# Graph attention with a memory layer on one core: edge ranks and places formed one projection earlier, and the first four permutation groups in a PSUM bank of their own

## The reference

```python
def gnn(n_f, ...):                       # n_f: layer-normed x, 256 x 1024, 8192 edges src, dst
    feat = concatenate([n_f[edge_src], n_f[edge_dst]], axis=1)
    e_hh = relu(feat[:128] @ W_hh + b_hh)
    e_oo = relu(feat[128:768] @ W_oo + b_oo)
    e_ho = relu(feat[768:] @ W_ho + b_ho)          # 7424 edges
    logit = (concatenate([e_hh, e_oo, e_ho]) @ W_a + b_a)[:, 0]
    m = segment_max(logit, edge_dst, 256)
    ex = exp(logit - m[edge_dst])
    alpha = ex / segment_sum(ex, edge_dst, 256)[edge_dst]
    z_f = segment_sum(alpha[:, None] * n_f[edge_src], edge_dst, 256)
    nf2 = concatenate([n_f, z_f], axis=1)
    return concatenate([relu(nf2[:64] @ W_hn + b_hn), relu(nf2[64:] @ W_on + b_on)])

x = x + gnn(layernorm(x), ...)
x = x + ffn(layernorm(x), ...)   # hash, top 4 of 256 memories, 1024 -> 32 -> 1024 each
```

## Time and profile before

| | before |
|---|---|
| median of 3 runs | 803.29 us (800.48 to 803.84) |
| the profiled execution's own time | 800.23 us |
| its span, first to last instruction | 798.5 us |
| outside the span | 1.7 us |
| granted TensorE clock, mean | 0.971 |
| PE busy | 741.0 us (93%) |
| DVE busy | 520.5 us (65%) |
| ACT busy | 347.9 us (44%) |
| POOL busy | 197.1 us (25%) |
| `lo` half, DVE L713 | x104, mean 2291 ns |
| `hi` half, ACT L538 | x104, mean 1910 ns |
| edge tile's dot, DVE L898 | x80, mean 1221 ns |

### The profile page before, as it was taken

How to read it: one execution, slowest core, us unless ns; L and a number is a source line. 1 busy time by engine, 2 the same in 40 slices (tenths; PEclk the granted TensorE clock), 3 DMA queues, 4 the chain that set the end, 5 groups by cost and what they waited for, 6 DMA issues and landing times.

```text
span 798.5 us, 9678 instructions
## 1 busy us (share of the span) xinstructions
PE 741.0 (93%) x3305; PEld 573.3 (72%) x3305; DVE 520.5 (65%) x832; ACT 347.9 (44%) x376; POOL 197.1 (25%) x345
## 2 busy tenths in 40 slices
PE   3999978797979998779999999999999999999998
PEld 3777756585555567548877787888888788888786
DVE  6884986596999999936488645445554544554543
ACT  3735576945634432113453443433443432444330
POOL 8200189998898804000000000000000000000000
PEclk9999999998999999868999999999999999999999
DMA  8783322241020013203823654566444466545411
GB/s 317 291 316 118 134 105 106 106 147 65 1 106 2 2 47 122 106 1 136 284 108 105 214 182 143 197 210 210 142 173 154 161 210 210 184 137 191 149 75 53
DMA packets 50060, 114.22 MB, mean 143 GB/s; under 512 B 2246, under 2 KB 35398, under 8 KB 44907
## 3 DMA queue, kind: packets, MB, share of 16 engines
q1 hardware_dynamic: 49418, 112.95, 39.5%
q0 software_dynamic: 160, 0.66, 0.2%
q10 hardware_dynamic: 448, 0.20, 0.1%
HBM read 112.74 MB, written 1.05 MB: 143 GB/s over the span
## 4 chain that ended last, share of the span: by engine, by line
PE 60%; POOL 20%; DVE 11%; issue 6%; ACT 2%; DVEq 0%; POOLq 0%; ACTq 0%
PE ps L1161 17%; PE ps L1163 17%; PE ps L1162 17%; POOL peak L494 5%; POOL chunk_col L487 5%; POOL oh_src L496 4%; POOL pen L499 4%; DVE wlo L713 3%; PE ps L1131 2%; DVE oh_dst L990 1%; PE ps L1431 1%; PE ps L1464 1%; ACT whi L538 1%; PE ps L1152 1%; PE ps L1197 1%
## 5 line engine op out<-in xcount | busy, mean ns | idle before, releaser
L713 DVE TENSOR_TENSOR wlo<-raw,whi 128x2048 fp32r<-128x2048 f32 x104 | 235.5, 2291 | 86.1 <-ACT whi L538 85.3
L538 ACT ACTIVATE whi<-raw 128x2048 fp32r<-128x2048 f32 x104 | 195.9, 1910 | 105.8 <-PE ps L1163 101.3
L1161 PE MATMUL ps<-whi,nT_hi 128*128 128x512 f32 x424 | 172.5, 407 | 3.6 <-DVE wlo L713 2.4
L1163 PE MATMUL ps<-wlo,nT_hi 128*128 128x512 f32 x424 | 169.3, 399 | 0.0
L1162 PE MATMUL ps<-whi,nT_lo 128*128 128x512 f32 x424 | 168.8, 398 | 0.0
L898 DVE SCALAR_TENSOR_TENSOR ps<-ps,xt 128x1024 f32<-128x1024 f32 x80 | 97.7, 1221 | 11.4 <-PE ps L1197 6.6
L1161 PEld LDWEIGHTS ps<-whi,nT_hi 128*128 128x128 f32 x424 | 80.5, 190 | 24.7 <-DVE wlo L713 3.3
L1161 PE MATMUL ps<-whi,gT_hi 128*128 128x512 f32 x240 | 95.3, 397 | 0.0
L1163 PE MATMUL ps<-wlo,gT_hi 128*128 128x512 f32 x240 | 95.2, 397 | 0.0
L1162 PE MATMUL ps<-whi,gT_lo 128*128 128x512 f32 x240 | 95.1, 396 | 0.0
L1095 DVE TENSOR_TENSOR gw<-act_g,route 128x512 f32<-128x512 f32 x32 | 20.7, 689 | 114.0 <-ACT act_g L676 113.9
(11 more groups left out here) (234 smaller groups left out, 902.0 us busy)
## 6 DMA issues: line engine op xcount, KB each, us to landing
raw<-n_L_ffn_values_down_dram SPq DMA_DIRECT2D x16, 2048.0 KB, 8.2
raw<-in_L_ffn_values_up_dram SPq DMA_DIRECT2D x16, 2048.0 KB, 7.4
raw<-in_L_gnn_W_hh_dram SPq DMA_DIRECT2D x8, 1024.0 KB, 8.8
raw<-in_L_gnn_W_oo_dram SPq DMA_DIRECT2D x8, 1024.0 KB, 5.1
raw<-in_L_gnn_W_ho_dram SPq DMA_DIRECT2D x8, 1024.0 KB, 5.1
raw<-in_L_gnn_W_hn_dram SPq DMA_DIRECT2D x8, 1024.0 KB, 4.9
raw<-in_L_gnn_W_on_dram SPq DMA_DIRECT2D x8, 1024.0 KB, 4.9
xt<-in_x_dram SPq DMA_DIRECT2D x4, 512.0 KB, 5.0
```

Source lines behind the costliest of these rows:

```text
L538: nc.scalar.activation(half(whi, s, j, down), half(raw, s, j, down), ACT.Copy)\
L713: nc.vector.tensor_tensor(half(wlo, s, j, down), half(raw, s, j, down), half(whi, s, j, down).bitcast(F32), ALU.subtract)\
L1161: nc.tensor.matmul(o, a_hi, b_hi, start=start, stop=False)
L1163: return nc.tensor.matmul(o, a_hi, b_lo, start=False, stop=stop)
```

## The change

`rank_edges` and `count_buckets` move up in `project(1, 0)`, after steps 3 and 1; `rank_rows` and `places` move up on their engines, between the halves of `hi(0, 3)` and `lo(0, 3)`. Groups 0 to 3 of the permutation run in `project(1, 1)`, into bank 3, after a wait that its four tables have been read. A new instruction on VectorE, `decode_early`, copies them to the new SBUF tile `part_idx`, and TensorE's second head tile, which overwrites bank 3, waits for that (`part_out`). Head tile i is followed by group i + 3 instead of i - 1; `project(2, 0)` has groups 9 to 14 after its steps 0 to 5. `decode` adds `part_idx` in place of copying. GpSimd makes the head destinations of tiles 3 to 5 behind its groups 5 to 7 instead of ahead of groups 1 to 3. `table_lo(1, 1)` is cut in two with a group's rows between, and the halves of `hi` and `lo` of (0, 4) and (0, 5) are interleaved with groups.

```diff
@@ gpsimd
             for n in range(CHUNKS):
                 if n >= 2:
                     pool.wait_ge(permuted, n - 1)
-                if 1 <= n <= HEAD - 3:
-                    head_destinations(n + 2)
...
                 last.then_inc(srccol_ready, 1)
+                if EARLY + 1 <= n < EARLY + HEAD - 2:
+                    head_destinations(n - 2)
@@ scalar
             hi(1, 2)
+            hi(0, 3, parts=(0,))
             rank_rows()
-            hi(0, 3)
+            hi(0, 3, parts=(1,))
+            destination_columns(0)
+            destination_columns(1)
             table_hi(1, 0)
             hi(1, 3)
-            hi(0, 4)
+            hi(0, 4, parts=(0,))
+            destination_columns(2)
+            hi(0, 4, parts=(1,))
+            destination_columns(3)
             table_hi(1, 1)
-            for n in range(HEAD + 1):
+            destination_columns(4)
+            destination_columns(5)
+            hi(1, 4)
+            for n in range(6, 13):
                 destination_columns(n)
-                if n == 1:
-                    hi(1, 4)
-            for n in range(HEAD + 1, HEAD + 5):
-                destination_columns(n)
-            hi(0, 5)
-            for n in range(HEAD + 5, CHUNKS):
-                destination_columns(n)
+            hi(0, 5, parts=(0,))
+            destination_columns(13)
+            hi(0, 5, parts=(1,))
+            destination_columns(14)
             table_hi(2, 0)
@@ vector
-                nc.vector.tensor_copy(slot_idx16[:], values)
-                nc.vector.tensor_copy(slot_idx[:], values).then_inc(decoded, 1)
+                nc.vector.tensor_tensor(slot_idx16[:], values, part_idx[:], ALU.add)
+                nc.vector.tensor_tensor(slot_idx[:], values, part_idx[:], ALU.add).then_inc(decoded, 1)
+
+            def decode_early():
+
+                dve.wait_ge(permuted, EARLY)
+                nc.vector.tensor_copy(part_idx[:].rearrange("p a w -> p (a w)"), bank(3)[:, 0:2 * WN]).then_inc(part_out, 1)
...
             bucket_counts()
-            lo(0, 3)
+            lo(0, 3, parts=(0,))
+            places()
+            lo(0, 3, parts=(1,))
+            chunk_rows(0)
+            chunk_rows(1)
             table_lo(1, 0)
             lo(1, 3)
-            places()
             head_onehot(1)
             head_onehot(2)
-            chunk_rows(0)
-            chunk_rows(1)
-            table_lo(1, 1)
+            chunk_rows(2)
+            chunk_rows(3)
+            table_lo(1, 1, (0, 1))
+            chunk_rows(4)
+            table_lo(1, 1, (2, 3))
+            decode_early()
             lo(0, 4)
             for i in range(1, HEAD):
                 edge_tile(i, pair_of(i))
                 if i + 2 < HEAD:
                     head_onehot(i + 2)
-                chunk_rows(i + 1)
+                chunk_rows(i + 4)
             lo(1, 4)
-            for n in range(HEAD + 1, HEAD + 5):
+            for n in range(10, 13):
                 chunk_rows(n)
-            lo(0, 5)
-            for n in range(HEAD + 5, CHUNKS):
-                chunk_rows(n)
+            lo(0, 5, parts=(0,))
+            chunk_rows(13)
+            lo(0, 5, parts=(1,))
+            chunk_rows(14)
             decode()
@@ tensor
-                    last = nc.tensor.matmul(bank(6)[:, 0:2 * WN], chunk_row[:, n % 2, j % CHUNK, :],
-                                            chunk_col[:, n % 2, j % CHUNK, :], start=j == 0, stop=j == JT - 1)
+                    last = nc.tensor.matmul(bank(3 if n < EARLY else 6)[:, 0:2 * WN], chunk_row[:, n % 2, j % CHUNK, :],
+                                            chunk_col[:, n % 2, j % CHUNK, :], start=j in (0, EARLY * CHUNK),
+                                            stop=j in (EARLY * CHUNK - 1, JT - 1))
...
+                if k == 1 and h == 0 and c == 1:
+                    count_buckets()
                 if k == 1 and h == 0 and c == 3:
-                    count_buckets()
-                if k == 1 and h == 0 and c == 6:
                     rank_edges()
-                if k == 2 and h == 0:
-                    permute(HEAD - 1 + c)
+                if k == 1 and h == 1 and c == 1:
+                    pe.wait_ge(tablo_ready, 4)
+                    permute(0)
+                if k == 1 and h == 1 and c == 3:
+                    permute(1)
+                if k == 2 and h == 0 and EARLY + HEAD - 1 + c < CHUNKS:
+                    permute(EARLY + HEAD - 1 + c)
...
+                        if k == 1 and (t, c) == (0, C - 1):
+                            permute(2)
+                        if k == 1 and (t, c) == (1, C - 3):
+                            permute(3)
...
                 pe.wait_ge(headdst_pool, i)
+                if i == 2:
+                    pe.wait_ge(part_out, 1)
...
                 gather_head(i)
-                permute(i - 1)
+                permute(EARLY - 1 + i)
             pe.wait_ge(dot_done, HEAD - 1)
             project(2, 0)
-            for n in range(HEAD - 1 + C, CHUNKS):
-                permute(n)
```

More of the change, by code:

```diff
@@ L58 @@
 REGS = 8
+EARLY = 4
 ROW = 80
@@ L173, in gnn_ffn @@
             chunk_gap = sb("chunk_gap", [P, CHUNK, WN], F16, edge)
+            part_idx = sb("part_idx", [P, 2, WN], F16, edge)
         pen_head = segall
@@ L272, in gnn_ffn @@
         permuted = sem("permuted")
+        part_out = sem("part_out")
         decoded = sem("decoded")
@@ L557, in _, with table_hi @@
             hi(0, 2)
-            def table_hi(k, h):
-                for t in range(NT):
+            def table_hi(k, h, tiles=range(NT)):
+                for t in tiles:
                     if t == 0:
@@ L886, in _, with table_lo @@
             lo(0, 2)
-            def table_lo(k, h):
+            def table_lo(k, h, quarters=range(4)):
                 tab = (tab_src, tab_dst)[h]
-                for q in range(4):
+                for q in quarters:
                     at, b = STACK_HI[q], STACK_BLOCK[q]
```

## The result

The changed kernel takes 795.31 us (794.19 to 795.58, four runs) against 803.13 (800.48 to 803.84) for the kernel before: a ratio of 0.9906, interval 0.9882 to 0.993. Run again for the experiments (`e1_after`), it was 794.32 against 804.69, ratio 0.9878, interval 0.9858 to 0.9897. Forecast: 794, range 788 to 800, faster.

What follows compares the result with a forecast made beforehand. The prediction took project(2, 1), not decoded, to move the end. Terms: -1.1 + 3.5 + 5.1 = 7.5, + 1.7 clock = 9.2 us; 791.0 against the profiled run, 794.1 against the median, so 794, range 788 to 800.

Steps and rivals of the forecast that it cites:

- What bounded: Whole kernel: GpSimd writing chunk_col from 119.5 to 153.6 us; the end moves with project(2, 1), not with decoded.
- Sorting: First projection: ranks and places move up, so edges are sorted at 69.2 us instead of 93.4.
- Second projection: From 72.2 us: four early groups added, first head starts at 97.7, 1.1 us later than before.
- Heads: Head tiles with their groups: 26.2 us instead of 29.7, 3.5 gained, a stall of 3.4 and a half clock staying.
- Third projection: project(2, 0) with groups 9 to 14: 25.8 us instead of 30.9, 5.1 gained, the new 2.0 inside.
- Clock: Start of project(2, 1): half clock at 158.9 to 162.3 goes with the idle time, 1.7 us gained.
- idle terms: Second projection, heads and third projection together: -1.1 + 3.5 + 5.1 = 7.5 us gained.
- the new 2.0: Third projection, near 130 us: TensorE waits 2.0 us for chunk_rows(10), which stands behind lo(1, 4) on VectorE.
- Rival 1: Clock falls again in the third projection, at project(2, 1)'s start or elsewhere: 7.5 us gained, 795.8; chance 0.15.
- rival 2: After head 2: 3.4 us stall brings no half clock at 111 (1.7), later stages lose one: 790 to 792; chance 0.15.
- Rivals 3 to 5: VectorE bounding the tables, 797 to 801, 0.12; late sorting, 804 and more, 0.04; edges not ready earlier, inside that 0.04.
- rival 3: Third projection: VectorE's queue makes group 13 or 14 slip 2 to 3 us each; gain 2 to 6; chance 0.12.

Runs made afterwards that it cites:

- e3_bias_spread: Changed kernel with the eight bias matmuls of project(1, 1) spread over steps 4 to 7 of project(1, 0); 794.09 us, ratio 0.9872.
- e6_after_pool: Changed kernel with one more GpSimd instruction per group, writing a tile nobody reads; 799.57 us, ratio 0.9943.
- e4_sorted_early: Kernel before with only ranks and places formed early, no group permuted early; 803.80 us, ratio 1.0004.
- e2_lo_early: Changed kernel with lo(0, 4) moved ahead of table_lo(1, 1) on VectorE; 789.39 us, ratio 0.9814.
- e7_decode_late: Changed kernel with three extra VectorE reductions between the last group and the decoding; 792.43 us, ratio 0.9853.
- e9_both_lo_early: Changed kernel with lo(0, 4) early and first halves of hi(1, 4) and lo(1, 4) between the destination tables' halves; 787.75 us, ratio 0.9801.
- e10_dest_first: Changed kernel with GpSimd's head destinations of tiles 3 to 5 ahead of its columns 5 to 7; 797.98 us, ratio 0.9927.
- e11_two_early: Changed kernel with two groups instead of four in project(1, 1), groups 7 to 14 in project(2, 0); 793.29 us, ratio 0.9886.
- e5_before_pool: Kernel before with one more GpSimd instruction per group, writing a tile nobody reads; 811.12 us, ratio 1.0092.

## Why the prediction was right

**What bounded.** Right. `chunk_col` on GpSimd left the chain, one instruction a group more cost the kernel before 6.6 us, and the end moved with `project(2, 1)` and not with `decoded`: `decoded` came 10 us sooner, the first dot 7.1. That is a tenth more than the 7 below which the prediction was to count as wrong, and 2 us short of the 9.2 forecast.

**Sorting.** The edges were sorted at 69.7, for 69.2 forecast.

**Second projection**, -1.1. It was -2.9: first head at 99.46 for 97.7, the term that was sized worst. 0.5 of the miss is the wait for `tablo_ready`, taken as 0.2, which is 0.72 where the clock holds (`e1_after`); sorting ended 0.5 late, and the columns stand in front of the tables. 0.7 is the half clock in 74.6 to 78.0, which no step had. The other 0.6 is in small pieces; 0.2 of it lie ahead of the projection (bias matmuls at 72.49, before at 72.26).

**Heads**, +3.5. Right to a tenth, 26.2, with the wait of 3.4 (it was 3.23) ended by `chunk_row`, the half clock behind it, and 0.53 at 104.50 for the 0.5. Both mechanisms are shown by undoing them: `lo(0, 4)` moved takes away wait and half clock, destinations moved back bring the old waits back.

**Third projection**, +5.1. 25.9 for 25.8; the new 2.0 is 1.83, the decoding at 146.7 five us before it is asked for. The prediction had GpSimd lose only group 11 to the `lo` pair. It lost the last column of group 10 as well, done at 133.15, and the wait fits because VectorE's rows, at 133.48, came a little later still.

**Clock**, +1.7. The half clock at 158.9 is gone, `project(2, 1)` takes 24.7 for 24.5. But the one at 74.6 came, 0.7 net, so in the profiled pair the term is 0.8, and the dot moved by 7.1, not 9.2. Over many runs the term is larger than I gave it. Runs of the kernel before on the chips of the experiments stand mostly at a mean clock of 0.963 to 0.967 and 803 to 806 us; those few at 0.971 took 800.6 to 800.9. The new kernel is mostly at 0.969 to 0.974, and its two runs at 0.971 took 793.5 and 794.2. At the same clock the change is worth some 6.4 to 7.4 us (the idle terms were 7.5), and the other 3 to 4 of the 10.4 in `e1_after` go with a higher mean clock; no trace of before at 0.963 to 0.967 was kept, so where its clock fell is not shown. The profiled execution of before had a high clock for that kernel. That I set the sum against it, and then moved the result up to the median, made 794 come out close. That closeness is in part luck: the idle terms were 1.2 too large in the profiled pair, the clock term about 2 too small over the runs beside `e1_after`, and the gain by medians was 7.8 us in the first runs and 10.4 in the second, for 9.2 forecast.

**Rivals.** Rival 1 is what the profiled execution shows, by its words "or once more elsewhere": its 7.5 us and 795.8 stand beside 7.1 and 795.31, though the half clock fell where it had not looked. Its other place, behind the new wait of 2.0, shows in `e3_bias_spread` (the fall at 133 behind 1.95). Half of rival 2's condition, the wait of 3 us without a half clock at 111, was met in two variants (3.08 in `e3_bias_spread`, 3.10 in `e6_after_pool`), and the clock fell elsewhere in both, so no time was gained by it. Rivals 3 to 5 did not occur; `e4_sorted_early` shows what is near to 5: sorted early, no early groups, no gain.

**What was argued wrongly though the number held.** "Only GpSimd pays, and early, where its groups have 5 us of slack", and the 3 us of slack a group in rival 3. The first half is right: the changed trace's `lo` pair beside GpSimd takes 4.49, and GpSimd's four destinations 6.42 under it for 2.47 without it. (By the Trainium skill, "SBUF — State Buffer", Terms, the loser of the shared port pair is fully blocked; the trace agrees: the column of 128.01 lasts 5.14 us, past the end of the `lo` pair at 132.75.) The second half is not. By 0.57 us a group the kernel loses 5 to 6 us. Slack counted at 2.5 against 3.07 us a group holds in the third projection alone: in the heads GpSimd has none (5.0 against 4.0), and the count says nothing of which columns fall under a `lo` pair. In the changed kernel one did. With all four the wait of 1.83 was 3.69 (`e6_after_pool`), which would have made the third term 1.9 smaller. The forecast stood closer to that edge than it said: by the rows, 0.3 us more of lateness on GpSimd were free, and from there on it would have gone into the wait.

## What to carry to other kernels

When three engines feed small groups to a fourth, the gain is in the place where the groups can start, and a sorted input earlier is worth nothing until the groups move too. What holds such groups up is long instructions ahead of or beside them in another queue: lay the long ones (here `lo` pairs of 4.5 us) between things that the waiting engine doesn't need next, in halves if need be. Probe slack by adding a small cost to each group before relying on it, and look whether the feeding engine works without a gap anywhere: there every small cost is passed on, and here it pushed a whole group under a long instruction, for a wait 1.9 to 2.2 us longer with a longer half clock behind it.

## What was not expected of the hardware

The granted clock fell to half at 74.6 behind a stretch in which TensorE was busy for 24.30 of 24.30 us, and in `e2_lo_early` at 149.4 with TensorE busy throughout ahead of it. Busy times, columns as for the stages, first of the changed kernel, then of `e2_lo_early`:

```profile
74.60:78.00 3.40, 3.40 (x9) 2.70 (x9) 2.01 (x2) 3.35 (x5) 2.16 (x4) 0.51 0.39 164
112.20:115.60 3.40, 3.40 (x11) 2.63 (x10) 3.15 (x12) 3.25 (x11) 3.40 (x7) 0.50 0.07 27
```

```profile
143.30:146.70 3.40, 3.40 (x16) 2.61 (x14) 0.13 (x1) 1.16 (x2) 2.96 (x8) 1.00 0.32 133
149.40:152.80 3.40, 3.40 (x10) 2.63 (x9) 3.28 (x3) 3.38 (x3) 3.14 (x6) 0.50 0.00 0
```

What the falls at 74.6 and 149.4 both follow is the block of eight bias matmuls of 5 rows with which `project(1, 1)` and `project(2, 1)` begin (72.49 and 146.77): the fall comes 2 to 4 us after its start. Behind the first block it is in seven traces (the changed kernel's, `e4_sorted_early`, `e6_after_pool`, `e7_decode_late`, `e9_both_lo_early`, `e10_dest_first`, `e11_two_early`) and missing in six with the same block (`e1_after`, of the same kernel, among them). Behind the second it is in two (`e2_lo_early`, and `e7_decode_late` at 154.1) of the ten traces that reach it without a wait. Where it followed the leftover groups, with TensorE busy for only 0.7 to 0.8 of the last 3.7 us (before, `e4_sorted_early`, `e5_before_pool`), the fall is in all three; where it followed a single wait of 0.71 for `decoded` (`e11_two_early`), it is missing. So the rows fit the prediction's cause for the half clock at 158.9, the dense idle time ahead of it, and show that it isn't the only one: a kernel without any idle time there still meets it at times. Whether the block brings it, and what decides between executions of one kernel, stays open.

Idle time and the fall go together no more simply than that: behind the wait for `chunk_row(5)` the clock fell after 3.23, 3.24 and 3.23 us (changed kernel, `e1_after`, `e7_decode_late`) and not after 3.08 and 3.10 (`e3_bias_spread`, `e6_after_pool`). Elsewhere it fell behind 1.95 (`e3_bias_spread`, at 133) and not behind 2.81 and 2.98 (`e11_two_early` at 110, `e5_before_pool` at 136).

Most of what runs of one kernel differ by goes with the mean clock. Of the 23 runs of before beside `e4_sorted_early`, the three at 0.971 took 800.60 to 800.67, the four at 0.963 took 805.5 to 805.9. Two profiled executions can differ by that much with the same code: compare their clocks first.
